# Graph attention: one wide copy and four transposes for the inverse row sums, and the PSUM banks dealt out anew

## The reference, cut to what matters

```python
# x: (4, 512, 512), ctx: (4, 512, 128); H = 8 heads of 64; two gat_layers, one after the other, per batch
def gat_layer(x, adj, W, a_self, a_neigh, b):
    feat = einsum('nf,hfo->hno', x, W)
    e = leaky_relu(attn_self[:, :, None] + attn_neigh[:, None, :], 0.2)
    e = e + -1e10 * (1.0 - adj)            # adj is layernorm(x) of the batch: 512 x 512
    alpha = softmax(e, axis=-1)
    out = einsum('hnm,hmo->hno', alpha, feat) + b
    return elu(concat_heads(out))
x = x + gat_layer(gat_layer(ctx, layernorm(x), ...0), layernorm(x), ...1)
```

## Time and profile before

| what | us |
|---|---|
| median of 3 runs (2304.18 to 2306.5) | 2304.65 |
| the profiled execution's own time | 2300.46 |
| its span | 2298.7 |
| graph attention in it, about | 30 to 616 |
| busy over the span: PE, DVE, ACT, POOL | 1841.5, 1461.6, 1051.0, 881.0 |

### The profile page before, as it was taken

How to read it: one execution, slowest core, us unless ns; L and a number is a source line. 1 busy time by engine, 2 the same in 40 slices (tenths; PEclk the granted TensorE clock), 3 DMA queues, 4 the chain that set the end, 5 groups by cost and what they waited for, 6 DMA issues and landing times. The chain is left out here.

```text
span 2298.7 us, 33608 instructions
## 1 busy us (share of the span) xinstructions
PE 1841.5 (80%) x8271; PEld 904.8 (39%) x8272; DVE 1461.6 (64%) x3126; ACT 1051.0 (46%) x1893; POOL 881.0 (38%) x949
## 2 busy tenths in 40 slices
PE   5588766887547999999982298888889429999994
PEld 2243333434344555555542022222222414444442
DVE  5777766777585565565555377777775575555552
ACT  5577766777333332233223156666667422222221
POOL 5465665666303555555542111111111013444441
PEclk8799987999778999999995589999999759999997
DMA  4100211110254789878556911111111626998884
GB/s 138 51 38 38 64 66 56 38 38 29 92 186 113 174 185 235 211 185 209 113 87 184 169 35 52 52 51 50 50 50 33 218 86 179 227 229 230 231 210 110
DMA packets 202160, 275.34 MB, mean 120 GB/s; under 512 B 83500, under 2 KB 121868, under 8 KB 200972
## 3 DMA queue, kind: packets, MB, share of 16 engines
q1 hardware_dynamic: 156955, 171.18, 24.4%
q0 software_dynamic: 38544, 97.02, 20.9%
q10 hardware_dynamic: 6561, 5.98, 1.4%
HBM read 204.44 MB, written 73.37 MB: 121 GB/s over the span
## 5 line engine op out<-in xcount | busy, mean ns | idle before, releaser
L1891 DVE TENSOR_REDUCE a_negmax<-a_m 128x1 f32<-128x512 f32 x512 | 328.1, 686 | 102.8 <-PE a_m L1747 101.2
L283 POOL TENSOR_TENSOR g_near<-g_mask,g_tb 128x512 f32<-128x512 f32 x256 | 322.5, 1275 | 155.6 <-DVE g_emin L544 153.6
L1839 ACT ACTIVATE a_prob<-a_s 128x1024 f32<-128x1024 f32 x256 | 260.6, 1021 | 142.6 <-PE a_s L1758 134.5
L365 PE MATMUL g_pt<-g_ident,g_p 128*128 128x128 f32 x1024 | 186.0, 314 | 130.3 <-DVE g_pT L553 121.2
L1283 PE MATMUL f_gu_bank<-f_wgu,f_xT 128*128 x768 | 267.9, 492 | 6.8 <-issue 3.6
L1747 PE MATMUL a_m<-a_kT,a_qT 112*128 (+1 forms) x512 | 198.3, 398 | 83.4 <-DVE a_negmax L1891 39.0
L474 ACT ACTIVATE g_p<-g_e,g_emin 128x512 f32<-128x512 f32 x256 | 183.3, 716 | 121.9 <-DVE g_emin L544 119.9
L1249 POOL DMA_INDIRECT tokens<-f_y,f_ids x96 | 151.1, 1573 | 220.2 <-DMA tokens<-f_y,f_ids 173.5
L1283 PE MATMUL s_gu_bank<-s_wgu,s_xT 128*128 128x512 f32 x512 | 232.5, 597 | 2.3 <-ACT s_xT L1335 1.6
L365 PEld LDWEIGHTS g_pt<-g_ident,g_p 128*128 128x128 f32 x1024 | 127.5, 157 | 257.9 <-DVE g_pT L553 205.2
L544 DVE CUSTOM_DVE_ANT_0 g_e<-g_near,g_h 128x512 f32<-128x512 f32 x256 | 173.3, 677 | 60.6 <-ACT g_h L459 31.7
(11 more groups left out here) (295 smaller groups left out, 2807.3 us busy)
## 6 DMA issues: line engine op xcount, KB each, us to landing
s_wgu<-in_L_ffn_w_gate_up SPq DMA_DIRECT2D x32, 1024.0 KB
f_wgu<-in_L_ffn_gate_up_proj SPq DMA_DIRECT2D x32, 768.0 KB
s_wd<-in_L_ffn_w_down SPq DMA_DIRECT2D x32, 512.0 KB, 4.1
a_qT<-q_parts SPq DMA_DIRECT2D x224, 64.0 KB, 2.2
g_tb<-neighbours SPq DMA_DIRECT2D x8, 1536.0 KB, 7.7
f_wd<-in_L_ffn_down_proj SPq DMA_DIRECT2D x32, 384.0 KB, 5.4
q_parts<-p_part SPq DMA_DIRECT2D x48, 128.0 KB, 2.3
g_tb<-neighbours SPq DMA_DIRECT2D x8, 512.0 KB, 4.3
```

Of the source, the lines that this page charges most:

```text
L283: pool.tensor_tensor(near[:, n % LAG, :], mask[slot][:, local % NT, :], t_all[k % SLOTS][:, local // NT, :], ALU.add).then_inc(near_ready, 1)
L365: last = nc.tensor.transpose(pt_bank[n % PT_BANKS][:, c, :], prob[:, n % LAG, c * P:(c + 1) * P], ident[:, :])
L1839: nc.scalar.activation(prob[n % QR][:, :, :], s_bank[n % RING][:, :, :], ACT.Exp).then_inc(p_ready, 1)
L1891: V.tensor_reduce(negmax[k % RING][:, st, head:head + 1], m_bank[n % RING][:, :], X_AXIS, ALU.max, negate=True).then_inc(m_read, 1)
```

## The change

Four parts. (1) The inverse row sums: GpSimd copies the 8 columns into a 128 x 512 tile `g_rw`, each repeated 64 times (`spread_sums`, at its step 6, after the mask tile of that step), and TensorE transposes its four blocks at step 3, in place of 8 matmuls at step 2. (2) The probabilities' transposes get three PSUM banks in place of two. (3) The preparation gets one bank in place of two: its rows go one unit earlier (VectorE 15 and 17, TensorE 16), and the features are in units 18 and 19, 21 and 22, 24 and 25, 27 and 28 (two matmuls a unit in layer 1; in layer 0 one in the second of them), each tile only after ScalarE has copied the one before, at 20, 23, 26 and 29. (4) For phase 0 the square root of the mask comes ahead of all the feature copies on ScalarE.

```diff
-    H_BANKS, PT_BANKS = 2, 2
+    H_BANKS, PT_BANKS = 2, 3
-    PREP_FIRST, PREP_FEAT = 10, 15
+    PREP_FIRST, PREP_ROWS, PREP_FEAT = 10, 15, 18
+        rwide = sb("g_rw", [P, RING, NT, 2, F_OUT])
-        prep_bank = [stack.enter_context(nc.psum_tensor(f"g_f{i}", [P, D], FP32)) for i in range(2)]
+        prep_bank = stack.enter_context(nc.psum_tensor("g_f", [P, D], FP32))
...
+                def spread_sums(pr):
+                    pool.wait_ge(rinv_ready, pr + 1)
+                    if pr >= RING:
+                        pool.wait_ge(r_ps, pr - RING + 1)
+                    pool.tensor_copy(rwide[:, pr % RING, :, :, :], bass.AP(rinv, pr % RING * PAIR, [[RING * PAIR, P], [1, NT], [NT, 2], [0, F_OUT]])).then_inc(rwide_ready, 1)
...
                         if 0 <= t < NT:
                             mask_tile(m, t)
+                    if n >= PAIR and n % PAIR == 6 and n // PAIR <= ALL_PAIRS:
+                        spread_sums(n // PAIR - 1)
...
-                    f = n - PREP_FEAT
-                    if 0 <= f < NT * NT and (layer or f % NT == 0):
-                        t, c = divmod(f, NT)
-                        if c == 0 and t == 1:
+                    t, part = divmod(n - PREP_FEAT, 3)
+                    if 0 <= t < NT and part < 2:
+                        if part == 0:
                             pe.wait_ge(s_ready, k + 1)
-                        if c == 0 and t >= 2:
-                            pe.wait_ge(feat_ready, k * NT + t - 1)
...
+                            pe.wait_ge(feat_ready, k * NT + t)
+                        for c in range(part * KC // 2, (part + 1) * KC // 2):
...
-                    if step == 2:
-                        pe.wait_ge(rinv_ready, pr + 1)
+                    if step == 3:
+                        pe.wait_ge(rwide_ready, pr + 1)
...
-                        for u in range(PAIR):
-                            t, hh = divmod(u, 2)
-                            last = nc.tensor.matmul(r_bank[hh * F_OUT:(hh + 1) * F_OUT, t, :],
-                                                    bass.AP(rinv, pr % RING * PAIR + hh * NT + t, [[RING * PAIR, P], [0, F_OUT]]), ident[:, :],
-                                                    start=True, stop=True)
+                        for t in range(NT):
+                            last = nc.tensor.transpose(r_bank[:, t, :], rwide[:, pr % RING, t, :, :].rearrange("p h o -> p (h o)"), ident[:, :])
...
-                    t, rest = divmod(n - PREP_FEAT - NT, NT)
-                    if rest == 0 and 0 <= t < NT:
+                    t, part = divmod(n - PREP_FEAT, 3)
+                    if part == 2 and 0 <= t < NT:
                         act.wait_ge(feat_ps, k * NT + t + 1)
```

More of the change, by code:

```diff
@@ L323, in prepare @@
                         for t in range(NT):
-                            last = nc.tensor.transpose(prep_bank[1][:, t * P:(t + 1) * P], ctx_sb[slot][:, t, :], ident[:, :])
+                            last = nc.tensor.transpose(prep_bank[:, t * P:(t + 1) * P], ctx_sb[slot][:, t, :], ident[:, :])
                         last.then_inc(xt_ps, 1)
@@ L330, in prepare @@
                         pe.wait_ge(xt_ready, batch + 1)
-                        nc.tensor.matmul(prep_bank[0][0:2 * H, :], wa[:, 0, :], xT[:, 0, :], start=True, stop=True).then_inc(stT_ps, 1)
+                        nc.tensor.matmul(prep_bank[0:2 * H, :], wa[:, 0, :], xT[:, 0, :], start=True, stop=True).then_inc(stT_ps, 1)
                     if layer == 1 and 0 <= m < KC:
@@ L337, in prepare @@
                         pe.wait_ge(h_ready, (k - 2) * PAIRS + m + 1)
-                        last = nc.tensor.matmul(prep_bank[0][0:2 * H, :], wa[:, m, :], xT[:, m, :], start=(m == 0), stop=(m == KC - 1))
+                        last = nc.tensor.matmul(prep_bank[0:2 * H, :], wa[:, m, :], xT[:, m, :], start=(m == 0), stop=(m == KC - 1))
                         if m == KC - 1:
                             last.then_inc(stT_ps, 1)
-                    if n == PREP_FEAT + 2:
+                    if n == PREP_ROWS + 1:
@@ L343, in prepare @@
                         pe.wait_ge(stT_ready, k + 1)
                         for t in range(NT):
-                            last = nc.tensor.transpose(prep_bank[0][:, t * H:(t + 1) * H], stT[k % SLOTS][0:H, t * P:(t + 1) * P], ident[0:H, 0:H])
+                            last = nc.tensor.transpose(prep_bank[:, t * H:(t + 1) * H], stT[k % SLOTS][0:H, t * P:(t + 1) * P], ident[0:H, 0:H])
                         last.then_inc(s_ps, 1)
-                    f = n - PREP_FEAT
-                    if 0 <= f < NT * NT and (layer or f % NT == 0):
-                        t, c = divmod(f, NT)
-                        if c == 0 and t == 1:
+                    t, part = divmod(n - PREP_FEAT, 3)
@@ L351, in prepare @@
+                    if 0 <= t < NT and part < 2:
+                        if part == 0:
                             pe.wait_ge(s_ready, k + 1)
-                        if c == 0 and t >= 2:
-                            pe.wait_ge(feat_ready, k * NT + t - 1)
-                        wf = w1[:, c, :, :] if layer else w0[:, :, :]
-                        last = nc.tensor.matmul(prep_bank[(t + 1) % 2][:, :], xT[:, c, t * P:(t + 1) * P],
-                                                wf.rearrange("p h o -> p (h o)"), start=(c == 0), stop=(c == KC - 1))
@@ L357, in prepare @@
-                        if c == KC - 1:
-                            last.then_inc(feat_ps, 1)
+                            pe.wait_ge(feat_ready, k * NT + t)
+                        for c in range(part * KC // 2, (part + 1) * KC // 2):
+                            wf = w1[:, c, :, :] if layer else w0[:, :, :]
+                            last = nc.tensor.matmul(prep_bank[:, :], xT[:, c, t * P:(t + 1) * P],
+                                                    wf.rearrange("p h o -> p (h o)"), start=(c == 0), stop=(c == KC - 1))
+                            if c == KC - 1:
+                                last.then_inc(feat_ps, 1)
@@ L460, in relu @@
                                          bias=s_high[k % SLOTS][:, t, h:h + 1]).then_inc(high_ready, 1)
-                for n in range(PREP_FIRST, PREP_FEAT + NT + 1):
+                for n in range(PREP_FIRST, PREP_FEAT):
                     prepare(0, n)
                 root(0)
-                for n in range(PREP_FEAT + NT + 1, UNITS):
+                for n in range(PREP_FEAT, UNITS):
                     prepare(0, n)
@@ L587, in _ @@
                 dve.sem_inc(wa0_done, 1)
-                prepare(0, PREP_FEAT + 1)
+                prepare(0, PREP_ROWS)
                 mask_statistics(0)
-                prepare(0, PREP_FEAT + 3)
+                prepare(0, PREP_ROWS + 2)
                 mask_variance(0)
```

13 lines of the change are left out of this document (7 added, 6 removed).

## The result

| | median of runs, us | profiled span, us | last pair's reciprocal, us |
|---|---|---|---|
| before | 2305.57 (4 runs) | 2298.7 | 604.48 |
| after | 2338.64 (2335.87 to 2343.06, 4 runs) | 2337.3 | 637.48 |

The changed kernel is slower: ratio 1.0138, 95% interval 1.0121 to 1.0155, 33 us. The forecast was 20 us slower, 2325; the time lies in the stated range (2298 to 2342), though 1.6 us above the range that the forecast gave its own case (2313 to 2337). Graph attention itself, up to the last reciprocal, is 33.0 us later.

A forecast was written before the change was run, and what follows sets the result against it. No engine fills graph attention, so waits make it, with TensorE the bound in phases 1, 2, 5 and 6. Summed: -16.5 + 0 + 14 + 4.9 + 18 = +20.4, 2320.9 us profiled, 2325 for runs; range 2298 to 2342.

The forecast's parts named there:

- its own case: Whole kernel: the forecast's sum holds, 2325 us for the runs, range 2313 to 2337; chance 0.52.
- Direction: Whole kernel: the change makes it slower, chance 0.73.
- the mask units: Phases 0, 3 and 4, units 20 to 23: GpSimd's copy waits behind VectorE's mask tile, 14 us lost (11 to 16).
- The start: Ahead of unit 0: phase 0's features take turns in one bank, so the relu starts 4.9 us later.
- The third bank: Transposed probabilities: transposes then wait for ScalarE alone, stalls shorten by 1.1 us each, 16.5 us gained together.
- The packing at 0: Features in one bank in TensorE-bound phases 1, 2, 5, 6: four stretches counted at 0 (6 less to 8 more).
- The clock at +18: Products with only transposes ahead meet TensorE's slow clock: 13 pairs at 1.2 us plus 2.4, together 18 (0 to 30).
- the saving of shorter sums: Four transposes for 8 matmuls: 6 us less over 12 TensorE-bound pairs, taken back by the later features.
- the clock holds: Rival: transposes of a busy TensorE keep its clock at 1.00, clock loss 0, mask loss 11.4: 2304.5 us; chance 0.16.
- All slow: Rival: TensorE-bound stretches partly at half clock too, 8 us in packing and 30 in clock: 2345 us; chance 0.08.
- The other side: Rival: TensorE's lateness is all, the third bank takes 40 us from the waits on it: 2283.5 us; chance 0.11.
- The mask units don't bind: Rival: GpSimd's copy is served earlier, so the mask term is 2 us, not 14: 2313 us; chance 0.13.

The follow-up runs named there:

- x1: The changed kernel with GpSimd's wide copy in mask units moved from unit 22, behind the mask tile, to unit 20, ahead of the first mask tile: 2320.12 us.
- x6: The changed kernel with phase 0's features of tiles 1 to 3 in the three banks of the transposed probabilities, free at that time: 2334.64 us.
- x2: The changed kernel with two banks for the transposed probabilities in place of three, one bank left unused: 2370.45 us.
- x5: The changed kernel with the old 8 matmuls for the sums at step 2, no GpSimd copy, and two banks for the transposed probabilities: 2350.48 us.
- x3: The changed kernel with the old 8 matmuls for the sums at step 2 and no GpSimd copy; one preparation bank and the third bank stay: 2320.08 us.
- x8: The changed kernel with the last feature tile's second half at unit 30 in place of 28, its copy at 31 in place of 29: 2333.40 us.
- x4: The kernel before with only the four transposes at step 3 and GpSimd's copy, ahead of the mask work; banks and preparation as before: 2316.27 us.
- x7: x4 with one ordinary matmul ahead of the sums' four transposes in 20 of the 32 pairs: 2329.48 us.
- x10: x4 with the sums' transposes still at step 3, but ahead of that unit's transposed probabilities in place of behind them: 2301.40 us.
- x9: x4 with the sums' transposes back at step 2, where the matmuls of before stood: 2306.51 us.
- x11: The changed kernel with the edits of x1, x6 and x8 together, and the sums' transposes at step 2: 2318.42 us.
- x12: x10 with the old matmuls at step 2 for 12 pairs (last of each phase, phase 7, third of phase 4): 2297.91 us.

## Why the prediction was right, and where it was not

The direction and the largest single loss were read correctly. That the time lies in the range is in part luck: the two halves of its sum were wrong by some 27 and 14 us, with opposite signs.

- **Direction, and the mask units: right.** Chain, place and size (14 counted, 16.0 measured, 17.4 by x1) hold; TensorE was at half clock there (1.92 for the feature matmul), which the sum had taken midway. Half of the whole loss is this.
- **The start: right.** 4.9 counted and measured; x6 takes 4.75 of it back.
- **The third bank: right in sign, half in size.** −16.5 counted, −31.8 (x2) and −30.4 (x5 against x3) measured. I had counted stalls of the kernel before; but the bank is needed most by the stretches that the packing makes, and by my rule these stood at 0. 14 us of its worth lie there (TensorE-bound pairs, x5 against x3).
- **The packing at 0: wrong, the largest error.** One bank for the preparation costs 47 us without the third bank, 42 beside the start. Together with it the change's second part costs 15 us (x3), where the prediction had −11.6. The failed step is the count that put four stretches at 0. Shown: that it is this part (x3, x5), and that the place of the last tile is some of it (x8). In the TensorE-bound pairs TensorE was busy 192.7 of 210.1 us before and is 185.3 of 222.2 in the changed kernel: it is no longer full, it waits. Read from the trace alone: the feature packs on the path, ScalarE's waits for them (41 to 61 us), and VectorE's wait for the self terms at unit 15, 15.3 us in 4 waits. For the last no run was made, none has the new units with two preparation banks, and how the 42 us split stays open.
- **The clock at +18: wrong in size.** The mechanism is there, and the slow products come about as counted: their busy time rose from 126.4 to 138.6 us. The timeline of the changed kernel has 62 rows of eight products, and 13 of them are over 2.05 us (two before), by 0.95 us over 1.94 on the mean, where 13 at 1.2 were counted. But not all of this is paid for: in phase 0's last pair the product takes 3.68, and the pair is 0.77 us shorter than before. And x1 and x3, which differ in the sums and not in the mask units, have equal times: by pairs the transposes, with their later step, cost 4.1 us in first pairs and 2.4 in phase 7, and give back 8.7 elsewhere. I had set the saving of shorter sums to 0 by giving it to the packing. One of the 13, in phase 7:

```profile
595.03 2.68 PE L404 MATMUL g_o<-g_pT,g_feat 128*64 128x512 f32 x8
```

It is 0.74 us longer than 1.94, where 1.2 was taken. By the Trainium skill ("TensorE: Matmul & The Clock Gate", Part 4: PE-mode transpose) transposes don't count as work for the clock. The runs agree in part: in phase 7 the product behind transposes alone took 2.40 us in x4, behind an ordinary matmul and transposes 1.94 in x7. But in x10, in the first pair of phase 3, the granted clock goes from 0.50 back to 1.00 at 249.9 us with nothing but transposes on TensorE since 243.2, and the product takes 1.94; so the measurement does not bear the statement out as it stands.

- **The step later: missed.** The prediction moved the sums from step 2 to 3 and priced it only in mask units. With two banks the place behind unit 3's transposes in place of ahead of them costs 8 to 15 us (x4 against x9 and x10); with three, ScalarE waits 7.5 us for the sums in all once the copy is early (x1), and x11 finds nothing to gain. The prediction's price for the clock would have fitted x4 by accident.

So 20.4 against 33 us is a smaller error than its parts: the second part was 27 us too cheap (−11.6 in place of 15), the first 14 too dear (32 in place of 18).

The rivals: "the clock holds" is refuted by the products' 138.6 us, though its 0 is nearer than my 18 to the 6.5 us that x1 pays over x3 in first pairs and phase 7. "All slow", at 2345, is closer to the measured time than the forecast, but not by its terms: the packing cost far more than its 8 us and the clock less than its 30, and the TensorE-bound stretches kept 0.94 to 0.97 of full clock (0.97 to 1.00 before). "The other side" had its finger on the right place, TensorE's lead, and the third bank did take 30 us; it fell because one bank for the preparation cost more. "The mask units don't bind" is refuted by x1.

## What to carry to other kernels

Taking a buffer from one stage to give it to another is two changes: run one without the other where the banks allow it, since here +47 and −31 looked like 0 and −16. Where an instruction is moved, look at what it stands behind in its engine's queue and at who copies its result: the same four transposes ahead of or behind another group were 8 to 15 us apart. And a copy put on an idle engine is hidden only where that engine has its lead; the three pairs in which it did other work cost half of the loss.

## What the runs showed of the hardware

GpSimd's copy out of a broadcast costs as its one-input work does, 0.61 us for 128x512 in the earlier trace rows; in the changed kernel:

```profile
L279 POOL COPY g_rw<-g_ri 128x512 f32<-128x512 f32 x32 | 20.0, 625 | 1.6 <-DVE g_ri L568 1.6
```

TensorE's clock rises at different moments over the same instructions. Before and x5 have one program in phase 7. From a reciprocal to 5.6 us behind it this pair's rows agree within 0.01 us, L383 included (1.98). Then eight transposes take 1.24 us before and 1.97 in x5, and the product 1.94 and 2.17. Before, and then x5:

```profile
578.70 1.24 PE L365 MATMUL g_pt<-g_ident,g_p 128*128 128x128 f32 x8
```

```profile
625.25 1.98 PE L382 MATMUL g_r<-g_ident,g_ri 128*64 128x128 f32 x16
627.15 1.97 PE L364 MATMUL g_pt<-g_ident,g_p 128*128 128x128 f32 x8
629.05 2.17 PE L396 MATMUL g_o<-g_pT,g_feat 128*64 128x512 f32 x8
```

The pair is 0.97 us longer for it, and between x9 and x10 such a pair differs by 2.27 us. So one or two us in one pair are not evidence, and some of x12's pairs may be no more than this.

TensorE's clock can come back with transposes alone: in x10 three first pairs (phases 3, 4 and 7) have eight transposes of 2.32 us and four of 1.06 at the slow level, then a product of 1.94, with no ordinary matmul between. In the earlier trace rows, with 0.20 us between groups of four, it stayed at 0.50.

The 5.7 us behind the stage: from the last reciprocal to the end of the span it is 1691.6 to 1694.7 us in the three kernels with the old sums alone (before, x3, x5), and 1697.9 to 1700.9 in the eleven others. The code there is the same. The profiled executions of these three were also below the medians of their own kernels (by 5.1, 1.3 and 2.7 us), while that of the changed kernel was 0.5 above; the medians of before and after differ by 33.1 us, as much as the stage alone. So the scatter between executions can make most of it. No run was made on it, and the cause is not shown.
